# Shared-expert blocks ahead of the routing counts in a two-best expert stage

## Chip, cores and metric

One core of a Trainium2 chip runs the whole program. The metric is device time in microseconds of one execution. TensorE (PE), VectorE (DVE), ScalarE (ACT) and GpSimd (POOL) each run an instruction stream of their own and meet at semaphores; SyncE (SP) only issues transfers.

## What is computed

The program is an eight-block network on 2048 tokens of width 128. The change is inside its sixth block, a mixture of experts with the two best of eight experts for each token and one shared expert for all tokens. Cut to what matters:

```
logits = rms_normalised(x) @ router_w.T;  topk_p, topk_i = top_k(softmax(logits), 2)
rw     = topk_p / sum(topk_p)                         # the two weights of a token
sel    = tokens that chose an expert, in token order; capacity 320 a expert
eout   = (silu(xg @ rg) * (xg @ ru)) @ rd             # xg: the rows of an expert
routed = scatter-add of eout * weight back to the tokens
shared = (silu(x @ sg) * (x @ su)) @ sd               # sg, su: 128 x 1024, sd: 1024 x 128
out    = shared + routed                              # then x + out, layer norm
```

## The kernel before

`stage_top2_experts` (L2799) is one block of five hand-written streams, one to an engine, between two barriers. What order an engine works in is the order of its code; nothing is scheduled by a tool. `s.name` are semaphores that count up, and `at(i, c)` is the value after item c of turn i.

**Routing on DVE.** `choose` (lines L1943 to L1947) finds the best expert, then the second best, each as a chain of five small operations linked by a semaphore. `hot` (L3004) is the 0/1 table of choices, 128 partitions by 128 (expert, tile). PE multiplies it by two constant matrices (L2861, L2862, results in banks 2 and 1) and so gets each token's count within its expert. DVE turns the counts into slots (L1961, L1962, L3010 to L3014; the last one is `scatter`) and then into the weights (`gap`, `acc`, `share`, L3015 to L3026), for which POOL brings the reciprocal root `rms` and ACT one Exp (L2936).

**Rows by slot.** ACT copies the tokens into `x_with_id` (L2934, four copies of 128x1024). When `scatter` is there, POOL issues 32 indirect transfers (L3104), which send each token's row to its two slots in memory, and after every eighth it waits for those so far. SP then loads the rows back by expert (L3124, five transfers), POOL takes the row numbers out of them (`ids`, L3108) and PE transposes them (L2892, 20 products).

**The shared expert** works on pairs of 256-token batches, 512 tokens, pair i of four. A pair has eight blocks c. For a block, PE makes a gate product and an up product (L2881, 128x128 by 128x512) in banks 3 or 4 and 5 or 6, by c % 2. ACT applies Silu to the gate (`shared_gate`, L2948), DVE multiplies it by the up product (`shared_hid`, L3036). PE may start block c when DVE has done block c-2, since then the banks are free; block 0 of a pair waits for block 7 of the pair ahead. After blocks 0 and 1 of a pair, PE does `shared_down` of the pair ahead (L2872 and L2873, four groups) and ACT copies its results to `shared` (L2940). Three pairs (`FIRST = 3`) run before the row transposes and the routed experts (L2902, L2852), the fourth after them. Both wait forms are in two lines:

```
pe.wait_ge(s.s_hid.sem, s.s_hid.at(i, max(0, c - 1)))     # before the two products of block c
dve.wait_ge(s.s_silu.sem, s.s_silu.at(i, c + 1))          # before the multiplication of block c
```

PE begins with the count products, then the shared expert. ACT begins with the four copies, then the Exp, then Silu. DVE begins with all of the routing, weights included, and only then multiplies for the shared expert.

## Time and profile before

| | us |
|---|---|
| median of 3 runs (lowest, highest) | 1695.76 (1693.24, 1698.86) |
| the profiled execution, its own time | 1698.1 |
| its span, first to last instruction | 1696.3 |
| the changed block, in that span | 1316.2 to 1490.5 |
| PE busy in that block | 155.31 of 174.30 |

A row gives the time an instruction starts, how long it lasts, the engine and line, what it writes and reads, and in brackets how long its engine stood idle before it and who released it. PE rows of one product in 32-bit floats are two records (x2), and the next product may start before the last record's end, so the pace is read from start to start. The granted clock is a share of 2.4 GHz: 1.00 is 2.4 GHz, 0.50 is 1.2 GHz.

### The profile page before, as it was taken

What the parts mean: (1) busy time and instruction counts of PE and PEld (TensorE: products, weight loads), DVE (VectorE), ACT (ScalarE), POOL (GpSimd) and SP (SyncE); (2) the same over time, 40 slices, a digit from 0 to 9 for tenths busy, and PEclk for the clock granted to TensorE, in tenths of its full rate; (3) what the DMA queues carried; (4) which work ended last, traced back from release to release, by engine and by line L of the source; (5) the groups of instructions that cost most, each with busy time, mean ns of one, the idle gap of its engine ahead of it and who ended that gap; (6) DMA issues with size and microseconds to landing.
All of it is one profiled execution on the core that took longest, in us unless ns stands there. A gap on an engine that the chain in (4) does not pass through costs nothing. (4 is left out here: it accounts for less than half of the span.)

```text
span 1696.3 us, 30747 instructions
## 1 busy us (share of the span) xinstructions
PE 1483.6 (87%) x11059; PEld 1085.3 (64%) x11059; DVE 1009.1 (59%) x2372; ACT 854.9 (50%) x1876; POOL 672.6 (40%) x779
## 2 busy tenths in 40 slices
PE   4589999899887999996849999899998899879996
PEld 3256676566774677675737877877877467635554
DVE  6656647666476799994045554366645412546665
ACT  5455555655547877772524444544444323225552
POOL 3397715977133677872130000100003522123334
PEclk8789999999998899997959999999998899969998
DMA  7300000000204765616243000000000110200000
GB/s 217 98 14 14 13 14 1 14 13 19 89 1 62 87 73 81 80 41 139 74 126 93 1 1 1 1 2 1 1 1 1 35 48 20 62 4 2 2 2 26
DMA packets 80943, 66.58 MB, mean 39 GB/s; under 512 B 28283, under 2 KB 67242, under 8 KB 80814
## 3 DMA queue, kind: packets, MB, share of 16 engines
q1 hardware_dynamic: 71198, 57.24, 16.4%
q0 software_dynamic: 2688, 5.53, 1.1%
q10 hardware_dynamic: 6928, 2.12, 0.6%
q8 instruction: 78, 1.28, 0.3%
q14 instruction: 51, 0.42, 0.1%
HBM read 48.89 MB, written 11.71 MB: 36 GB/s over the span
## 5 line engine op out<-in xcount | busy, mean ns | idle before, releaser
L1557 POOL TENSOR_TENSOR inject<-delta_x,b_rows 128x512 f32<-128x512 f32 x128 | 160.2, 1277 | 65.1 <-DVE delta_x L1854 37.5
L1881 DVE TENSOR_TENSOR_SCAN state<-bank,inject 128x512 f32<-128x512 f32 x128 | 150.1, 1209 | 7.5 <-issue 5.2
L2314 POOL TENSOR_TENSOR ve<-mv,eps 128x1 f32<-128x1 f32 x32 | 6.1, 190 | 336.0 <-DVE mv L2462 336.0
L1786 ACT ACTIVATE bank<-delta,a_neg 128x255 f32<-128x255 f32 x256 | 108.9, 473 | 6.8 <-DVE state L1881 6.1
L2423 ACT ACTIVATE Z<-bank 128x512 f32<-128x512 f32 x64 | 34.7, 594 | 127.9 <-PE bank L2376 127.9
L2400 ACT ACTIVATE U<-bank 128x512 f32<-128x512 f32 x128 | 74.7, 593 | 41.1 <-PE bank L2337 40.1
L1661 PEld LDWEIGHTS bank<-tabs,by_token 128*128 128x128 f32 x512 | 68.7, 198 | 25.0 <-issue 15.1
L632 POOL TENSOR_TENSOR rotated<-rot_cos,rot_sin 128x512 f32<-128x512 f32 x52 | 65.8, 1269 | 46.0 <-DVE rot_sin L1001 46.0
L3613 DVE TENSOR_REDUCE top<-bank 128x2 f32<-128x512 f32 (+1 forms) x96 | 61.9, 686 | 35.6 <-PE bank L3317 17.8
L1797 ACT ACTIVATE by_token<-bank,c_cols 128x256 f32<-128x256 f32 x128 | 53.7, 470 | 50.5 <-PE bank L1635 50.2
L638 POOL TENSOR_TENSOR inv_norm<-sum_sq,neghalf 128x16 f32<-128x16 f32 x26 | 76.1, 2925 | 3.9 <-POOL sum_sq L636 0.8
L3214 POOL TENSOR_SCALAR_AFFINE_SELECT prob<-prob 128x512 f32<-128x512 f32 x64 | 39.1, 634 | 92.5 <-ACT prob L3519 92.5
L1665 PE MATMUL bank<-x_work,tabs 128*128 128x512 f32 x128 | 74.2, 663 | 0.0
L1661 PE MATMUL bank<-tabs,by_token 128*128 128x128 f32 x512 | 70.3, 282 | 0.0
L998 DVE TENSOR_TENSOR rot_cos<-bank,rope 128x512 f32<-128x512 f32 x64 | 43.9, 686 | 36.9 <-ACT squares L876 27.9
L3519 ACT ACTIVATE prob<-bank 128x384 f32<-128x384 f32 x128 | 53.2, 500 | 24.4 <-PE bank L3340 24.4
L681 PE MATMUL bank<-wqkv,hT 128*128 128x512 f32 x112 | 57.8, 641 | 8.4 <-ACT hT L871 6.2
L876 ACT ACTIVATE squares<-bank 128x512 f32<-128x512 f32 x64 | 38.1, 598 | 46.6 <-PE bank L681 20.7
L3036 DVE TENSOR_TENSOR shared_hid<-shared_gate,bank 128x512 f32<-128x512 f32 x32 | 21.9, 688 | 56.7 <-PE bank L2881 55.9
L906 ACT ACTIVATE prob<-bank 128x512 f32<-128x512 f32 x64 | 34.7, 595 | 40.9 <-PE bank L728 40.7
L643 POOL TENSOR_TENSOR rotated<-rotated,inv_norm 128x512 f32<-128x512 f32 x52 | 53.2, 1044 | 2.0
L1635 PE MATMUL bank<-tabs,state 128*128 128x128 f32 x256 | 40.4, 282 | 11.7 <-DVE state L1881 8.8
(575 smaller groups left out, 4126.7 us busy)
## 6 DMA issues: line engine op xcount, KB each, us to landing
b_rows<-rows_dram SPq DMA_DIRECT2D x32, 512.0 KB, 9.0
v<-v SPq DMA_DIRECT2D x32, 130.0 KB, 2.3
by_token<-zero SPq DMA_DIRECT2D x8, 256.0 KB, 3.3
moe_w<-in_L_ffn_rg_dram SPq DMA_DIRECT2D x1, 2048.0 KB, 8.4
moe_w<-in_L_ffn_ru_dram SPq DMA_DIRECT2D x1, 2048.0 KB, 13.7
x_with_id<-by_token SPq DMA_DIRECT2D x16, 128.0 KB, 2.4
wqkv<-in_L_ffn_wqkv_dram SPq DMA_DIRECT2D x2, 768.0 KB
rows<-padded SPq DMA_DIRECT2D x5, 258.0 KB, 4.6
```

The source lines that it names most:

```text
L632: pool.tensor_tensor(rot[:, p, m, :], rc[:, m % 2, :], rs[:, m % 2, :], ALU.add).then_inc(s.added.sem, 1)
L638: pool.tensor_tensor(flat(rn), flat(ss), net.neghalf[:, 0:2 * LH], ALU.pow).then_inc(s.inv_norm.sem, 2)
L643: pool.tensor_tensor(of, of, rn[:, m, :].unsqueeze(2).to_broadcast([P, LH, LDH]), ALU.mult).then_inc(s.roped.sem, 1)
L681: pe.matmul(to, hT[:, p, tok(t)], w[:, j * INNER:(j + 1) * INNER], start=True, stop=True).then_inc(s.qk_ps.sem, 1)
L1557: pool.tensor_tensor(dB[:, n % R, :, :], dx[:, :, seq(n)], both(b_all[:, q % 4, n % CH, :]), ALU.mult).then_inc(s.inject.sem, 1)
L1661: last = pe.matmul(sum_bank(i)[:, c * L + t * P:c * L + (t + 1) * P], hcT[:, j % RT, t, c * P:(c + 1) * P], ident, start=(k == 0 and t == ...
L1665: last = pe.matmul(sum_bank(i)[:, :], ident, flat(hc[:, j % R, :, :]), start=False, stop=(k == NS - 1))
L1786: last = act.activation(dA[n % RD][:, c, 1:L], delta[:, c, i * L + 1:(i + 1) * L], ACT.Exp, scale=a_neg[:, c, k:k + 1])
L1797: last = act.activation(hcT[:, j % RT, t, :], turn_bank[:, t * 2 * P:(t + 1) * 2 * P], ACT.Copy, scale=c_cols[:, TPB * i + t, k:k + 1])
L1881: dve.tensor_tensor_scan(flat(h[:, n % R, :, :]), flat(dA[n % RD]), flat(dB[:, n % R, :, :]), 0.0, ALU.mult, ALU.add).then_inc(s.state.sem, 1)
L2400: act.activation(U[:, m % 2, 4 * (g - 1):4 * g, :], bank[n % 2][:, :].rearrange("p (h t) -> p h t", h=4), ACT.Copy)\
L3613: dve.tensor_reduce(to, M[u % 2].rearrange("p (c k) -> p c k", c=count), AX.X, ALU.max).then_inc(s.maxed.sem, 1)
```

## The change

On PE the two count products move from the front of the stream to between block 1 and block 2 of pair 0. On ACT the four row copies move behind the Silu of block 1 of pair 0, and the Exp behind the Silu of block 0 of pair 1. On DVE the multiplications of pair 0 are put into the routing: blocks 0 and 1 behind `hot`, blocks 2 and 3 behind the counts, blocks 4 to 7 behind `scatter`, and the weights come after all of pair 0. No computation is added or removed.

```diff
@@ -2855,11 +2855,13 @@
             @block.tensor
             def _(pe):
                 pe.wait_ge(net.ld_w3, net.w3_ready)
-                pe.wait_ge(s.tables.sem, s.tables.at(0, 1))
-                pe.wait_ge(s.hot.sem, s.hot.at(0, 1))
-                flat = hot[:, :, :].rearrange("p e t -> p (e t)")
-                pe.matmul(bank[2][:, 0:NT * E2], ones[:, :], flat, start=True, stop=True)
-                pe.matmul(bank[1][:, 0:NT * E2], before[:, :], flat, start=True, stop=True).then_inc(s.counts.sem, 1)
+
+                def count():
+                    pe.wait_ge(s.tables.sem, s.tables.at(0, 1))
+                    pe.wait_ge(s.hot.sem, s.hot.at(0, 1))
+                    flat = hot[:, :, :].rearrange("p e t -> p (e t)")
+                    pe.matmul(bank[2][:, 0:NT * E2], ones[:, :], flat, start=True, stop=True)
+                    pe.matmul(bank[1][:, 0:NT * E2], before[:, :], flat, start=True, stop=True).then_inc(s.counts.sem, 1)
 
                 def shared_down(p):
                     pe.wait_ge(s.s_hid.sem, s.s_hid.at(p, SC))
@@ -2876,6 +2878,8 @@
                 def shared_expert(first, end):
                     for i in range(first, end):
                         for c in range(SC):
+                            if i == 0 and c == 2:
+                                count()
                             pe.wait_ge(s.s_hid.sem, s.s_hid.at(i, max(0, c - 1)))
                             for w, to, done in ((net.sg, gate_bank(c), s.sg_ps), (net.su, up_bank(c), s.su_ps)):
                                 pe.matmul(to[:, :], w[:, c * P:(c + 1) * P], net.xT[:, 2 * i * L:2 * (i + 1) * L], start=True, stop=True).then_inc(done.sem, 1)
@@ -2928,12 +2932,11 @@
 
             @block.scalar
             def _(act):
-                for half in range(2):
-                    for c in range(2):
-                        of = net.x_tok[:, half * T // 2:(half + 1) * T // 2].rearrange("p (t d) -> p t d", d=D)
-                        act.activation(with_id[:, c, half * NT // 2:(half + 1) * NT // 2, 0:D], of, ACT.Copy).then_inc(s.with_id.sem, 1)
-                act.wait_ge(s.shifted.sem, s.shifted.at(0, 1))
-                act.activation(gap[:, :], gap[:, :], ACT.Exp).then_inc(s.exp.sem, 1)
+                def number_rows():
+                    for half in range(2):
+                        for c in range(2):
+                            of = net.x_tok[:, half * T // 2:(half + 1) * T // 2].rearrange("p (t d) -> p t d", d=D)
+                            act.activation(with_id[:, c, half * NT // 2:(half + 1) * NT // 2, 0:D], of, ACT.Copy).then_inc(s.with_id.sem, 1)
 
                 def keep_shared(i):
                     act.wait_ge(s.shared_ps.sem, s.shared_ps.at(i, 1))
@@ -2946,6 +2949,11 @@
                             act.wait_ge(s.sg_ps.sem, s.sg_ps.at(i, c + 1))
                             act.wait_ge(s.s_hid.sem, s.s_hid.at(i, max(0, c - 1)))
                             act.activation(sgate[:, c % 2, :], gate_bank(c)[:, :], ACT.Silu).then_inc(s.s_silu.sem, 1)
+                            if i == 0 and c == 1:
+                                number_rows()
+                            if i == 1 and c == 0:
+                                act.wait_ge(s.shifted.sem, s.shifted.at(0, 1))
+                                act.activation(gap[:, :], gap[:, :], ACT.Exp).then_inc(s.exp.sem, 1)
                             if c == 1 and i > first:
                                 keep_shared(2 * i - 2)
                                 keep_shared(2 * i - 1)
@@ -2993,6 +3001,14 @@
                     ins.then_inc(s.v.sem, 1)
                     dve.wait_ge(s.v.sem, s.v.at(0, count[0]))
 
+                def shared_pair(i, first=0, end=SC):
+                    for c in range(first, end):
+                        dve.wait_ge(s.s_silu.sem, s.s_silu.at(i, c + 1))
+                        dve.wait_ge(s.su_ps.sem, s.su_ps.at(i, c + 1))
+                        if i >= 2:
+                            dve.wait_ge(s.shared_ps.sem, s.shared_ps.at(2 * (i - 1), 0))
+                        dve.tensor_tensor(shid[:, i % 2, c, :], sgate[:, c % 2, :], up_bank(c)[:, :], ALU.mult).then_inc(s.s_hid.sem, 1)
+
                 count_tables(dve, link, net, before[:, :], ones[:, :], keep[:, :, :], E2)
                 dve.nop().then_inc(s.tables.sem, 1)
                 by_tile = lambda ap: ap.rearrange("p e t -> p t e")
@@ -3002,16 +3018,19 @@
                 link(dve.scalar_tensor_tensor(rest[:, :, :], hot1, NEG, logits, ALU.mult, ALU.add))
                 choose(dve, link, rest[:, :, :], iota, tops[:, 1, :], eq[:, :, :], index[:, 1, :], hot2, E2)
                 dve.tensor_tensor(hot[:, :, :], hots[:, 0, :, :], hots[:, 1, :, :], ALU.add).then_inc(s.hot.sem, 1)
+                shared_pair(0, 0, 2)
                 trash = net.tab("trash").rearrange("p (k t) -> p k t", k=2)
                 link(dve.tensor_scalar(offset[:, :, :], index[:, :, :], float(C2), float(64 * C2 - 1), ALU.mult, ALU.add))
                 link(dve.tensor_tensor(offset[:, :, :], offset[:, :, :], trash, ALU.subtract))
                 dve.wait_ge(s.counts.sem, s.counts.at(0, 1))
                 counts_before(dve, link, pre[:, :, :], keep[:, :, :], bank[1][:, 0:NT * E2], bank[2][:, 0:NT * E2])
+                shared_pair(0, 2, 4)
                 link(dve.tensor_tensor(at_hot[:, :, :, :], hots[:, :, :, :], pre[:, :, :].unsqueeze(1).to_broadcast([P, 2, E2, NT]), ALU.mult))
                 link(dve.tensor_reduce(pos[:, :, :], at_hot[:, :, :, :].rearrange("p k e t -> p k t e"), AX.X, ALU.add))
                 link(dve.tensor_tensor(slot[:, :, :], pos[:, :, :], offset[:, :, :], ALU.add))
                 link(dve.scalar_tensor_tensor(offset[:, :, :], pos[:, :, :], float(C2), slot[:, :, :], ALU.is_le, ALU.mult))
                 dve.tensor_tensor(scatter[:, :, :], offset[:, :, :], trash, ALU.add).then_inc(s.slots.sem, 1)
+                shared_pair(0, 4, SC)
                 link(dve.tensor_tensor(gap[:, :], tops[:, 1, :], tops[:, 0, :], ALU.subtract))
                 link(dve.tensor_scalar(acc[:, :, :], pos[:, :, :], float(C2), None, ALU.is_le))
 
@@ -3026,16 +3045,7 @@
                     link(dve.tensor_tensor(p2, inv[:, :], acc[:, 1, :], ALU.mult))
 
                 weights()
-
-                def shared_pair(i, first=0, end=SC):
-                    for c in range(first, end):
-                        dve.wait_ge(s.s_silu.sem, s.s_silu.at(i, c + 1))
-                        dve.wait_ge(s.su_ps.sem, s.su_ps.at(i, c + 1))
-                        if i >= 2:
-                            dve.wait_ge(s.shared_ps.sem, s.shared_ps.at(2 * (i - 1), 0))
-                        dve.tensor_tensor(shid[:, i % 2, c, :], sgate[:, c % 2, :], up_bank(c)[:, :], ALU.mult).then_inc(s.s_hid.sem, 1)
-
-                for i in range(FIRST):
+                for i in range(1, FIRST):
                     shared_pair(i)
                 for e in range(E2):
                     for c in range(FC):
```

ScalarE holds one table of functions at a time; where the order of functions changes, the compiler places the loads (ACT_TABLE_LOAD) anew. Below, the start of the block on ACT before, in program order. `x_with_id` are the row copies, `gap` the Exp.

```order
L2934 ACTIVATE x_with_id<-x_tok 128x8x128 x4
L2936 ACTIVATE gap<-gap 128x16
L2948 ACT_TABLE_LOAD
L2948 ACTIVATE shared_gate<-bank 128x512 x10
L2940 ACTIVATE shared<-bank 128x256 x2
```

And the same place of the changed kernel:

```order
L2951 ACT_TABLE_LOAD
L2951 ACTIVATE shared_gate<-bank 128x512 x2
L2939 ACTIVATE x_with_id<-x_tok 128x8x128 x4
L2951 ACTIVATE shared_gate<-bank 128x512 x7
L2956 ACT_TABLE_LOAD
L2956 ACTIVATE gap<-gap 128x16
L2951 ACT_TABLE_LOAD
L2951 ACTIVATE shared_gate<-bank 128x512
L2943 ACTIVATE shared<-bank 128x256 x2
```

One table load has become three: the first stands at the very start of the block, the other two enclose the Exp, between blocks 0 and 1 of pair 1.

On PE, the start of the block in the changed kernel (before, L2861 and L2862 stood ahead of the first product of L2881):

```order
L2885 MATMUL bank<-xT,sg 128x512
L2885 MATMUL bank<-xT,su 128x512
L2885 MATMUL bank<-xT,sg 128x512
L2885 MATMUL bank<-xT,su 128x512
L2863 MATMUL bank<-hot,ones_158 128x128
L2864 MATMUL bank<-hot,before 128x128
L2885 MATMUL bank<-xT,sg 128x512
L2885 MATMUL bank<-xT,su 128x512
```

Four products of pair 0 now stand ahead of the counts, which still wait for `hot`.

On DVE, from `hot` on in the changed kernel (before, L3036, the multiplication, came only behind the last `share`, 24 times in a row):

```order
L3020 TENSOR_TENSOR hot<-hots 128x128
L3010 TENSOR_TENSOR shared_hid<-shared_gate,bank 128x512 x2
L3023 TENSOR_SCALAR offset<-index 128x32
L3024 TENSOR_TENSOR offset<-offset,tabs 128x32
L1961 SCALAR_TENSOR_TENSOR pre<-keep,bank 128x128
L1962 TENSOR_TENSOR pre<-pre,bank 128x128
L3010 TENSOR_TENSOR shared_hid<-shared_gate,bank 128x512 x2
L3028 TENSOR_TENSOR at_hot<-hots,pre 128x256
...
L3032 TENSOR_TENSOR scatter<-offset,tabs 128x32
L3010 TENSOR_TENSOR shared_hid<-shared_gate,bank 128x512 x4
L3034 TENSOR_TENSOR gap<-tops 128x16
```

Four multiplications now stand ahead of `scatter`, and all eight of pair 0 ahead of the weights.

## Rows read from the trace of the kernel before

**Rows 1.** The page: span, and busy time of each engine.

```profile
span 1696.3 us, 30747 instructions
PE 1483.6 (87%) x11059; PEld 1085.3 (64%) x11059; DVE 1009.1 (59%) x2372; ACT 854.9 (50%) x1876; POOL 672.6 (40%) x779
```

**Rows 2.** Busy time of the engines and granted clock (PEclk), by stretches.

```profile
core 0: us, PE busy (x) PEld busy (x) DVE busy (x) ACT busy (x) POOL busy (x), PEclk, DMA share, GB/s
1316.20:1321.70 5.50, 0.00 (x0) 0.02 (x1) 4.66 (x19) 3.90 (x4) 3.25 (x2) 0.50 0.00 0
1321.70:1324.50 2.80, 2.79 (x5) 1.30 (x6) 2.28 (x7) 0.00 (x0) 0.00 (x0) 0.50 0.00 0
1324.50:1326.70 2.20, 2.20 (x6) 0.77 (x4) 1.59 (x9) 1.45 (x2) 1.14 (x1) 0.99 0.00 0
```

**Rows 3.** Timeline of PE: the block's start, pair 0, start of pair 1.

```profile
1321.71 0.27 PE L2861 MATMUL bank<-hot,ones 128*128 128x128 bf16 x1 [5.73 <-DVE hot L3004]
1321.87 2.02 PE L2881 MATMUL bank<-xT,sg 128*128 128x512 f32 x2
1323.69 1.46 PE L2881 MATMUL bank<-xT,su 128*128 128x512 f32 x2
1324.98 1.02 PE L2881 MATMUL bank<-xT,sg 128*128 128x512 f32 x2
1325.84 1.02 PE L2881 MATMUL bank<-xT,su 128*128 128x512 f32 x2
1328.19 1.13 PE L2881 MATMUL bank<-xT,sg 128*128 128x512 f32 x2 [1.33 <-DVE shared_hid L3036]
...
1339.61 1.12 PE L2881 MATMUL bank<-xT,sg 128*128 128x512 f32 x2 [0.85 <-DVE shared_hid L3036]
```

**Rows 4.** Timeline of ACT: the block's start.

```profile
1316.26 3.90 ACT L2934 ACTIVATE x_with_id<-x_tok 128x1024 f32<-128x1024 f32 x4 [0.77 <-PEq L2727]
1325.24 0.22 ACT L2936 ACTIVATE gap<-gap 128x16 f32<-128x16 f32 x1 [5.08 <-DVE gap L3020]
1325.47 1.28 ACT L2948 ACT_TABLE_LOAD   x1
1326.76 1.08 ACT L2948 ACTIVATE shared_gate<-bank 128x512 f32<-128x512 f32 x2
```

**Rows 5.** Timeline of DVE: from hot to the first multiplications.

```profile
1321.27 0.29 DVE L3004 TENSOR_TENSOR hot<-hots 128x128 bf16<-128x128 f32 x1
1322.19 0.42 DVE L1961 TENSOR_TENSOR_SCAN pre<-keep,bank 128x128 f32<-128x128 f32 x1 [0.31 <-PE bank L2862]
1322.97 0.42 DVE L3010 TENSOR_TENSOR at_hot<-hots,pre 128x256 f32<-128x256 f32 x1
1324.50 0.19 DVE L3014 TENSOR_TENSOR scatter<-offset,tabs 128x32 int32<-128x32 f32 x1
1327.45 1.28 DVE L3036 TENSOR_TENSOR shared_hid<-shared_gate,bank 128x512 f32<-128x512 f32 x2 [0.88 <-ACT shared_gate L2948]
```

**Rows 6.** Timeline of the next block's start, ACT and weight loads of PE.

```profile
1490.50 1.28 ACT L3493 ACT_TABLE_LOAD   x1 [0.27 <-PEq L2842]
1490.51 0.50 PEld L3280 LDWEIGHTS bank<-w_qkv,xT 128*128 128x128 f32 x2 [1.10 <-issue]
```

**Rows 7.** Timeline of PE: down products of pair 0, end of the third pair.

```profile
1343.15 1.95 PE L2872 MATMUL bank<-sd,shared_hid 128*128 128x128 f32 x16
...
1351.19 1.02 PE L2881 MATMUL bank<-xT,sg 128*128 128x512 f32 x2
...
1393.52 2.35 PE L2892 MATMUL bank<-tabs,rows 128*128 128x128 f32 x20
```

**Rows 8.** Timeline of POOL: first of 32 scatters, last, last row numbers.

```profile
1325.55 1.14 POOL L3104 DMA_INDIRECT padded<-x_with_id,scatter  x1 [4.58 <-DVE scatter L3014]
...
1368.77 0.96 POOL L3104 DMA_INDIRECT padded<-x_with_id,scatter  x1 [0.30 <-issue]
...
1379.67 0.19 POOL L3108 CAST ids<-rows 128x4 int32<-128x4 f32 x1 [0.65 <-DMA rows<-padded]
```

## The prediction, made before the change was run

> **What bounds the kernel now.** I read the page first: PE is busy for 1483.6 of 1696.3 us and is the busiest engine [rows 1], so a change pays if it closes a gap on PE and leaves PE's work as it is. Then the busy time by stretches at the start of the changed block. From 1316.2 to 1321.7 PE does nothing, while DVE is busy for 4.66 us with the choice of experts and ACT for 3.90 us with its copies; the granted clock is 0.50, the 1.2 GHz level [rows 2]. PE's timeline says what ends this: `hot`, after 5.73 us of idle [rows 3]. The next gap follows soon. The four products of blocks 0 and 1 begin at 1321.87, the last at 1325.84 and, at the pace of 0.86 us, it is done at 1326.70; then PE stands until 1328.19, waiting for `shared_hid` [rows 3]. ACT's timeline has the cause: Exp must wait for the routing until 1325.24, the Silu table comes behind it, and the first Silu starts at 1326.76 [rows 4]. From 1328.19 on PE works evenly: pair 1 starts at 1339.61 [rows 3], which is 11.42 us for the six blocks 2 to 7 and the hand-over to the next pair. A block is a gate and an up product of 0.86 us each; two blocks are 3.43 us of it, so four blocks with the hand-over are 7.99 us.
>
> Behind that the cover of the routed rows counts: PE wants them only at 1393.52 [rows 7], while the last row numbers are there at 1379.67 [rows 8]. There are 13.8 us of room.
>
> The number to follow through the change is therefore the start of pair 1. What it moves forward, the rest of the block should pass on: from there to the row transposes PE is the engine waited for.
>
> **PE, the first four products.** They no longer wait for `hot`. In the next block PE loads its first weights at 1490.51, with ACT's first instruction at 1490.50 [rows 6]; so I let PE start here with ACT, at about 1316.3 [rows 4]. Their length hangs on the clock. In the kernel before, PE starts at the low level; over its first 2.80 us the granted clock is 0.50, and in the next 2.20 us it is 0.99 [rows 2], which makes the four products last 4.83 us (1321.87 to 1326.70). When the rise comes if PE starts 5.5 us sooner, the trace doesn't show. The bounds: again 2.8 us after the start, so that they end at 1321.1; or not at all within them, so that all four run at twice 0.86 us, with the 0.1 us more that the first row shows, and end at 1323.2.
>
> **The counts.** `hot` ends at 1321.56 (1321.27 and 0.29), as before, since nothing ahead of it on DVE is touched. At the first bound PE waits for it for some 0.5 us, and the counts come at the same time as now. At the second bound they come 1.5 us later than now.
>
> **ACT.** The Silu table is loaded at once, 1316.3 to 1317.5 (1.28 us [rows 4]), and the first gate product ends at 1318.1 at the earliest, so this load is hidden. The Silu of block 1 needs the third product: it is done at 1321.1, at the second bound at 1322.3. Then come the four copies, 3.90 us [rows 4]: ACT is free for block 2 at 1325.0 or 1326.2. This is the new wait. Behind the copies on ACT stands the Silu of block 2, behind that its multiplication on DVE, behind that block 4 on PE, and the at_hot to `scatter` chain.
>
> **DVE.** Two multiplications of 1.28 us together [rows 5] end at 1322.9, two offset operations take 0.4, the count operations 0.78 (1322.19 to 1322.97 [rows 5]): 1324.1. Then DVE waits for ACT. Silu of block 2 takes 0.6 (1.08 for two, 0.48 apart), the multiplication 0.7 with its 0.1 us of hand-over: `shared_hid` of block 2 is there at 1326.4, at the second bound at 1327.6.
>
> **Sum for pair 0.** PE starts block 2 at 1322.3 when block 0 has been multiplied, blocks 2 and 3 take 3.4 us to 1325.8, then it stands 0.6 us and starts block 4 at 1326.4. Four blocks and the hand-over are 7.99 us, so pair 1 starts at 1334.4 in place of 1339.61: 5.2 us gained. At the second bound it is 1327.6 + 8.0 = 1335.6 and 4.0 us. Put as gaps: 5.7 us at `hot` and 1.5 us at the table go, 1.0 to 1.1 us come back at the copies and before the counts, and what the slow clock takes longer is the difference between the bounds.
>
> If the clock rises sooner than 2.8 us, the Silu of block 1 comes before 1321.1 and everything behind it too; the copies then end at 1324.2 or so, and the gain goes to about 5.9 us. I take 4.7 us, a little above the middle of 4.0 and 5.2, for that side.
>
> **Scatter.** The two further multiplications, blocks 2 and 3, now stand ahead of it. Block 3's ends at 1327.0; the chain from at_hot to `scatter` takes 1.72 us (1322.97 to 1324.69 [rows 5]), so `scatter` is ready at 1328.8 or, at the second bound, 1329.9, which is 4.1 to 5.2 us late. All 32 scatters of POOL move with it, and the five loads on SP's queue and the row numbers behind them: the last are there at 1384 to 1385. PE wants them at 1393.52 less the gain, 1388.8. Four to five of the 13.8 us of room are left; without them each us of lateness would cost one.
>
> **Exp and weights.** After pair 0 on DVE, at about 1334.4, `gap` needs some 0.6 us; ACT does the Silu of block 0 of pair 1 until about 1336.1, then a load, Exp at 0.22 and a load: 1338.9, and the Silu of block 1 ends at 1339.5. DVE's five weight operations, queued ahead of the multiplications of pair 1, end at about 1339.0, so block 1 is multiplied by 1340.3. PE has blocks 0 and 1 and then 8.04 us of down products (1343.15 to 1351.19 [rows 7]), now until 1346.0. The 2.8 us that ACT adds are hidden with 5.7 us to spare; without this cover they would cost 2.8 us.
>
> This is where a rule speaks against the change. The Trainium skill, page "ScalarE: Activation LUTs", section "What ACT_TABLE_LOAD costs", puts a switch at 2.66 us, with 1.38 us of draining on top of the load, and its rules for kernel authors ask for grouping by table. Here Exp ends at 1325.46, the load runs from 1325.47 to 1326.75 and Silu starts at 1326.76 [rows 4]: no draining shows. By the page the two loads around Exp would take 5.3 us in place of 2.6, the cover would shrink from 5.7 to 3.0 us, and the sum would be the same.
>
> **The sum.** The profiled execution took 1698.1 us, its span 1696.3 and 1.8 around it; less 4.7 that is 1693.4. It lies 2.3 us above the median of the runs, so against the median I forecast 1695.76 - 4.7 = 1691.1 us. The three runs lie 5.6 us apart, as much as the whole gain.
>
> **Rivals.** (a) As summed, gain 4.0 to 5.9 us, 1689.9 to 1691.8 us: 75%.
> (b) The change does less than it says, since the gain is swallowed behind pair 1 or PE does not really start with ACT: gain 0 to 3.5 us, time about 1694. For it: the room for the rows shrinks from 13.8 to about 4 us, and what else might hold PE at the block's start is hidden now by the wait for `hot`. Against it: the start of the next block, and the even pace of the scatters: 13%.
> (c) The gaps cost less than the rows of before suggest (copies overlap with Silu, clock up at once, later steps also gain): 6 to 7.5 us, about 1689: 7%.
> (d) Slower. The clock stays at the low level through all of pair 0, because PE now starts in the cold and then pauses at `hot`, at block 4 and at the hand-over. Twelve products after block 1, each 0.86 us longer, are 10.3 us; less the gain at the second bound of 4.0 that is 6.3 us lost, 1702. It turns the sign once the low level lasts over five of these products. Against it: the clock of before holds through the pause of 1.49 us at 1326.70, which the pace of 0.86 us afterwards shows: 5%.
>
> **Range and chances.** A change of 0.3%, 5.1 us, is about what a measurement tells from none; the border lies at 1690.7 and my forecast is just on the near side. Case (a) is split by it and by the spread of the runs, about 38 of its 75 points beyond the border and 37 within; (c) is faster; (b) is within; of (d) 4 points are slower. So 0.46 faster, 0.50 the same, 0.04 slower. For the range I take (a) and add the spread of a median of few runs, some 2 us each way, and the near part of (b) and (c): 1687.3 to 1694.8.
>
> **What the changed profile would show.** PE idle at the start under 0.5 us; the table load first on ACT; count products at 1321.7 to 1323.3 in place of 1321.71; PE waiting for `shared_hid` about 0.6 us before block 4; first scatter 4 to 5 us later; two table loads around Exp with no wait of PE behind; PE without a wait at the row transposes; pair 1 started at 1334.4 to 1335.6 and the block shorter by as much. The prediction is wrong if pair 1 starts sooner but the row transposes do not, if PE's first product starts well after ACT's first instruction, or if the granted clock is 0.50 beyond block 1.

## The result: 3.6 us less, and what the profile after shows

The changed kernel takes 1693.18 us, the median of 17 runs (1689.24 to 1695.32); the kernel before takes 1695.87 us in 17 runs (1693.09 to 1700.24). The ratio is 0.9979, with a 95% interval of 0.9971 to 0.9987: 3.6 us less, between 2.2 and 4.9. The two medians lie only 2.7 us apart, the two means 3.5; the gains given here by the ratio are not differences of medians. The forecast was 4.7 us less. Measured again (`e6_after_again` below) the ratio was 0.9971, 0.9957 to 0.9984, or 4.9 us less.

The profiled execution of after took 1689.24 us. The page's lines, beside [rows 1]:

```profile
span 1687.5 us, 30750 instructions
PE 1484.6 (88%) x11059; PEld 1085.6 (64%) x11059; DVE 1008.8 (60%) x2372; ACT 857.0 (51%) x1878; POOL 672.6 (40%) x779
```

PE has the same 11059 matmul records and is busy 1 us longer; ACT has the two table loads more and is busy 2.1 us longer. The span is 8.8 us shorter, and this must not be put down to the change: ACT's first instruction of the changed block stands at 1311.18, against 1316.26 before [rows 4], so 5.1 us of it were won ahead of any line that the change touches. In the profiles of this study the block begins anywhere from 1310.89 to 1318.72, with the same code ahead of it. So from here on each time in the block is read as a **distance from ACT's first instruction of the block**. The timeline of ACT, to be laid beside [rows 4] and, with its last line, [rows 6]:

```profile
1311.18 1.28 ACT L2951 ACT_TABLE_LOAD   x1 [0.81 <-PEq L2727]
1313.47 0.60 ACT L2951 ACTIVATE shared_gate<-bank 128x512 f32<-128x512 f32 x1 [1.01 <-PE bank L2885]
1316.59 0.60 ACT L2951 ACTIVATE shared_gate<-bank 128x512 f32<-128x512 f32 x1 [2.52 <-PE bank L2885]
1317.08 3.88 ACT L2939 ACTIVATE x_with_id<-x_tok 128x1024 f32<-128x1024 f32 x4
1320.87 1.07 ACT L2951 ACTIVATE shared_gate<-bank 128x512 f32<-128x512 f32 x2
...
1332.04 1.28 ACT L2956 ACT_TABLE_LOAD   x1
1333.34 0.21 ACT L2956 ACTIVATE gap<-gap 128x16 f32<-128x16 f32 x1
1333.57 1.28 ACT L2951 ACT_TABLE_LOAD   x1
1334.87 0.60 ACT L2951 ACTIVATE shared_gate<-bank 128x512 f32<-128x512 f32 x1
...
1481.15 1.28 ACT L3503 ACT_TABLE_LOAD   x1 [0.27 <-PEq L2842]
```

The load is the first thing on ACT now, and is over before the first gate product is. Between Silu of blocks 1 and 2 stand the four copies; until 1320.87 ACT can't take up block 2. The last line is the next block's first instruction: the block lasts 169.97 us in place of 174.24 [rows 4, 6], 4.27 less. PE's timeline, beside [rows 3, 7]:

```profile
1311.39 2.04 PE L2885 MATMUL bank<-xT,sg 128*128 128x512 f32 x2 [0.53 <-PEq L2727]
1313.23 1.91 PE L2885 MATMUL bank<-xT,su 128*128 128x512 f32 x2
1314.94 1.61 PE L2885 MATMUL bank<-xT,sg 128*128 128x512 f32 x2
1316.39 1.02 PE L2885 MATMUL bank<-xT,su 128*128 128x512 f32 x2
1317.24 0.22 PE L2863 MATMUL bank<-hot,ones 128*128 128x128 bf16 x1
...
1322.28 1.12 PE L2885 MATMUL bank<-xT,sg 128*128 128x512 f32 x2 [1.27 <-DVE shared_hid L3010]
...
1330.27 1.12 PE L2885 MATMUL bank<-xT,sg 128*128 128x512 f32 x2 [0.85 <-DVE shared_hid L3010]
...
1333.80 1.95 PE L2874 MATMUL bank<-sd,shared_hid 128*128 128x128 f32 x16
...
1341.84 1.02 PE L2885 MATMUL bank<-xT,sg 128*128 128x512 f32 x2
...
1384.17 2.35 PE L2896 MATMUL bank<-tabs,rows 128*128 128x128 f32 x20
```

The idle time in brackets on the first line is 0.53 us in place of 5.73. Read the starts of the next four lines against each other: 1.84, 1.71, 1.45 and 0.85 us apart, so PE goes from the slow pace to the fast one within the third product. After blocks 2 and 3 it waits 1.27 us for `shared_hid`: that is the wait put there by the copies. Pair 1 starts at 1330.27. The busy time by stretches (columns as in [rows 2]) has the clock to it:

```profile
1311.20:1315.70 4.50, 4.31 (x5) 1.83 (x6) 3.84 (x15) 1.86 (x2) 3.10 (x2) 0.50 0.00 0
1315.70:1317.30 1.60, 1.60 (x5) 0.67 (x4) 1.27 (x4) 0.71 (x2) 0.15 (x1) 0.87 0.00 0
1317.30:1322.20 4.90, 3.71 (x11) 1.45 (x9) 2.34 (x7) 4.64 (x6) 0.00 (x0) 1.00 0.00 0
```

The low level (0.50, 1.2 GHz) holds for all of the first row and, at a mean of 0.87, for 0.42 us of the second, so until 1316.12. That is 4.7 us after PE's start, where it was 2.8 us before [rows 2]; then comes 2.4 GHz, which stays through the wait at block 4. DVE and POOL, beside [rows 5, 8]:

```profile
1316.15 0.29 DVE L3020 TENSOR_TENSOR hot<-hots 128x128 bf16<-128x128 f32 x1
...
1317.52 0.69 DVE L3010 TENSOR_TENSOR shared_hid<-shared_gate,bank 128x512 f32<-128x512 f32 x1 [0.49 <-PE bank L2885]
...
1321.54 1.28 DVE L3010 TENSOR_TENSOR shared_hid<-shared_gate,bank 128x512 f32<-128x512 f32 x2 [2.24 <-ACT shared_gate L2951]
...
1324.27 0.19 DVE L3032 TENSOR_TENSOR scatter<-offset,tabs 128x32 int32<-128x32 f32 x1
```

```profile
1325.32 1.14 POOL L3114 DMA_INDIRECT padded<-x_with_id,scatter  x1 [9.46 <-DVE scatter L3032]
...
1378.01 0.19 POOL L3118 CAST ids<-rows 128x4 int32<-128x4 f32 x1 [0.64 <-DMA rows<-padded]
```

As distances, with the same rows of before:

| distance from ACT's first instruction, us | before | after | earlier by |
|---|---|---|---|
| PE's first product of block 0 | 5.61 | 0.21 | 5.40 |
| block 2 starts | 11.93 | 6.18 | 5.75 |
| block 4 starts | 15.47 | 11.10 | 4.37 |
| pair 1 starts | 23.35 | 19.09 | 4.26 |
| row transposes start | 77.26 | 72.99 | 4.27 |
| next block starts | 174.24 | 169.97 | 4.27 |
| first scatter | 9.29 | 14.14 | -4.85 |
| last row numbers | 63.41 | 66.83 | -3.42 |

The gain is 5.4 to 5.8 us while PE fills its idle time, loses 1.4 us in front of block 4, and from pair 1 on is carried without loss to the end of the block. Behind the block part of it is given back. From the next block's first instruction to the end of the span the kernel before has 205.80, 205.80 and 205.84 us in three profiles (with `e5` and `e9` below), the changed one 206.35 and 206.31 (with `e6`): 0.5 us more, with the same code. The granted clock over the first 50 us of this stretch is 0.75 in all three profiles of before and 0.70 in both of after. So 3.7 to 3.8 us of the 4.3 reach the end of the kernel, which fits the 3.6 of the ratio. That the clock costs these 0.5 us is not shown: `e7` has 0.80 there and yet 206.08 us.

### The profile page after: what moved, and what is told of

Its sections match the earlier page's. It is cut to its first block and busy times, and to the rows that moved or that the text cites. A ratio compares the mean times of both kernels' runs of the same rounds, so it can differ in the third digit from the quotient of the medians.

```text
span 1687.5 us, 30750 instructions
## 1 busy us (share of the span) xinstructions
PE 1484.6 (88%) x11059; PEld 1085.6 (64%) x11059; DVE 1008.8 (60%) x2372; ACT 857.0 (51%) x1878; POOL 672.6 (40%) x779
## 3 DMA queue, kind: packets, MB, share of 16 engines
q8 instruction: 78, 1.28, 0.3%
```

## The experiments

Theory A is the forecast's: the gain is PE's idle time at the block's start, less the wait at the copies, less what the low clock costs, with enough cover for the rows and for Exp. The rivals are that the gain is given back behind pair 1, by rows that come too late or by what ACT has to do there, or that one part of the change makes all of it. In the expectations of `e5` to `e9`, theories A and B are something else: whether a stop of ACT that the first four profiles show comes with the chip (A) or with the new orders (B). The kernels ran in three groups, each on one chip: the first four, then `e5` to `e8`, then `e9` to `e12`. Diffs are against the changed kernel.

**The first four** try each order by itself. `e1_counts_only` has PE's order of the changed kernel and leaves ACT's and DVE's as they were before:

```diff
             def _(act):
-                def number_rows():
+                for half in range(2):
...
+                act.wait_ge(s.shifted.sem, s.shifted.at(0, 1))
+                act.activation(gap[:, :], gap[:, :], ACT.Exp).then_inc(s.exp.sem, 1)
...
                 dve.tensor_tensor(hot[:, :, :], hots[:, 0, :, :], hots[:, 1, :, :], ALU.add).then_inc(s.hot.sem, 1)
-                shared_pair(0, 0, 2)
...
-                shared_pair(0, 2, 4)
...
-                shared_pair(0, 4, SC)
...
                 weights()
-                for i in range(1, FIRST):
+                for i in range(FIRST):
                     shared_pair(i)
```

> Only PE's stream is changed (four products of pair 0 ahead of the counts); ACT and DVE work in the order of before. Measure: the distance from ACT's first instruction of the block to the first product of pair 1, 23.35 us before and 19.09 us in the changed kernel. Theory (the idle time of PE at the start is worth nothing by itself, since block 2 waits for the first multiplication, which needs Silu, its table, Exp and the routing): distance 23.4 to 24.0, time as before or up to 0.7 us more, since the counts now wait for four products at the low clock. Rival (what counts is that PE's 5.7 us of idle time are filled): distance about 18, time 5 us less than before.

`e2_copies_two_and_two` makes two of the copies behind Silu of block 0 and two behind block 1:

```diff
-                def number_rows():
-                    for half in range(2):
+                def number_rows(halves):
+                    for half in halves:
...
-                            if i == 0 and c == 1:
-                                number_rows()
+                            if i == 0 and c < 2:
+                                number_rows((c,))
```

> The changed kernel, but ACT makes two of its four row copies behind the Silu of block 0, where it stood idle for 2.5 us, and two behind the Silu of block 1. Theory (the four copies in a row make PE wait 1.4 us at block 4): no wait of PE at block 4, distance 17.7 us (19.09 less 1.4), 1.4 us less than the changed kernel and 5.7 us less than before, ratio to before 0.9967. Rival (PE waits there for the multiplication behind the routing on DVE, or the slow clock is the bound): distance 19.1, the time of the changed kernel.

`e3_copies_first` has all four ahead of the first Silu, as before:

```diff
-                            if i == 0 and c == 1:
-                                number_rows()
...
+                number_rows()
                 shared_expert(0, FIRST)
```

> The changed kernel, but all four row copies ahead of the first Silu, and so ahead of its table load too. Theory (position of the copies): Silu of block 0 comes only 5.2 us after the block's start, block 2 begins 0.5 us later than in the changed kernel, but block 4 does not wait: distance 18.1 us, 1.0 us less than the changed kernel. Rival (copies don't matter): 19.1.

`e4_exp_in_pair_0` has Exp and the weights where half of pair 0 still has to be done, so that no down products cover the two table loads:

```diff
-                            if i == 1 and c == 0:
+                            if i == 0 and c == 3:
                                 act.wait_ge(s.shifted.sem, s.shifted.at(0, 1))
...
-                shared_pair(0, 4, SC)
                 link(dve.tensor_tensor(gap[:, :], tops[:, 1, :], tops[:, 0, :], ALU.subtract))
...
                 weights()
+                shared_pair(0, 4, SC)
```

> The changed kernel, but the weights on DVE come straight behind scatter, ahead of the multiplications of blocks 4 to 7, and Exp on ACT behind the Silu of block 3: the two table loads lose their cover of down products. Theory (loads of 1.28 us each, hidden only by that cover): Exp at 14.0 us from the start, Silu of block 4 at 15.5, block 6 on PE at 16.9 in place of 14.6: distance 21.4 us, 2.3 us more than the changed kernel. Rival 1 (a switch costs 2.66 us): 22.8 us. Rival 2 (the place of Exp does not matter): 19.1 us.

Measured, with the start of pair 1 as a distance:

| kernel | pair 1 | transposes | block | median, us | ratio to before |
|---|---|---|---|---|---|
| e1_counts_only | 25.84 | 81.34 | 178.31 | 1699.81 | 0.9964 (0.9950 to 0.9979) |
| e2_copies_two_and_two | 17.49 | 82.42 | 179.4 | 1699.83 | 0.9962 (0.9947 to 0.9978) |
| e3_copies_first | 18.0 | 81.32 | 178.29 | 1702.58 | 0.9980 (0.9963 to 0.9998) |
| e4_exp_in_pair_0 | 21.43 | 83.09 | 180.06 | 1699.90 | 0.9959 (0.9944 to 0.9974) |

The starts of pair 1 can be read; the rest can't. Those of `e2`, `e3` and `e4` are within some 0.2 us of what was expected; that of `e1`, 25.84, lies outside both its theory and its rival, and is taken up again with `e10`. Here the kernel before took 1705.96 us, 10 more than elsewhere, and in all four profiles the stretch from pair 1 to the transposes is 55.5 to 64.9 us long, where it is 53.9 in the profiles of before and after. ACT's and then PE's timeline of `e2_copies_two_and_two` show where:

```profile
1340.40 0.38 ACT L2943 ACTIVATE shared<-bank 128x256 f32<-128x256 f32 x1 [2.67 <-PE bank L2875]
1349.14 0.38 ACT L2943 ACTIVATE shared<-bank 128x256 f32<-128x256 f32 x1 [8.36 <-remote]
1350.58 0.60 ACT L2951 ACTIVATE shared_gate<-bank 128x512 f32<-128x512 f32 x1 [1.05 <-remote]
```

```profile
1344.10 1.02 PE L2885 MATMUL bank<-xT,sg 128*128 128x512 f32 x2
...
1352.10 2.08 PE L2885 MATMUL bank<-xT,sg 128*128 128x512 f32 x2 [4.40 <-DVE shared_hid L3010]
```

PE is done with all down products at 1344.10, and yet ACT takes up the last of their results only at 1349.14; `remote` is the trace's word for a releaser that it doesn't see. PE then waits 4.40 us and works on at the slow pace. Two explanations were open: a new order on ACT brings this about (theory B), or it belongs to the chip. So the kernels were run again elsewhere, beside unchanged ones.

**The changed kernel and the one before, again.** `e5_before_again` is the kernel before, `e6_after_again` the changed one, without an edit.

> The kernel before, unchanged, profiled again beside the others of this call. In the profiles of the first four experiments ACT stood still for 5 us or more around the copies of the shared results of pair 0, with PE's products long done, and the kernel before took 1706 us there against 1696 in its first runs. Theory A (this comes with the chip or the moment, not with the order of the work): the kernel before shows the same stop on such a chip, in the stretch from pair 1 to the row transposes, 53.9 us in its first profile and then about 60. Theory B (the changed orders bring it about): 53.9 us here, whatever the chip.

> The changed kernel, unchanged, again. Distance from ACT's first instruction of the block to the first product of pair 1: 19.1 us where the clock rises about 4.3 us after PE's start, 18.2 us if it rises after 2.8 us or less, 19.3 us if later. Time against before: by the distances 4.3 us less, ratio 0.9975. Theory A of the stop in ACT: from pair 1 to the transposes the same length as the kernel before has in this call. Theory B: longer than there.

Before: pair 1 at 23.35, transposes at 77.26, block 174.24 us, in one run of 1694.70 us. After: pair 1 at 19.00, transposes at 72.91, block 169.89, median 1692.90 against 1696.44, ratio 0.9971 (0.9957 to 0.9984). Between these profiles and the first ones PE's distances repeat to 0.1 us, while the whole kernel's time wanders by 5. So the gain in the block, 4.27 to 4.35 us, is known better from two pairs of profiles than from the timed runs. The clock rises 4.7 us after PE's start here too, and not after the expectation's 4.3, where the first row of the stretches above ends. The kernel before shows no stop of ACT on this chip, so theory A of the stop is left untried.

**Copies two and two, again.** `e7_copies_two_and_two_again` is the code of `e2`.

> Copies two and two, again. Distance 17.5 us as in the first look. By the distances 5.9 us less than before, ratio 0.9966, and 1.6 us less than the changed kernel of the same call. Theory B of the stop (an order that keeps ACT's copies away from block 4 brings it about): from pair 1 to the transposes 60 us or more where the changed kernel has 54.

Pair 1 starts at 17.34, the transposes at 71.26, the block lasts 168.24 us; median 1691.09, ratio 0.9960 (0.9947 to 0.9973). The stretch behind pair 1 is 53.92 us long again: ACT's long stop is gone with the same code, so the order alone does not cause it. ACT's timeline, then PE's:

```profile
1321.09 2.00 ACT L2939 ACTIVATE x_with_id<-x_tok 128x1024 f32<-128x1024 f32 x2
1323.47 0.60 ACT L2951 ACTIVATE shared_gate<-bank 128x512 f32<-128x512 f32 x1 [0.39 <-PE bank L2885]
1323.97 1.99 ACT L2939 ACTIVATE x_with_id<-x_tok 128x1024 f32<-128x1024 f32 x2
1325.86 0.59 ACT L2951 ACTIVATE shared_gate<-bank 128x512 f32<-128x512 f32 x1
```

```profile
1324.31 1.13 PE L2885 MATMUL bank<-xT,sg 128*128 128x512 f32 x2
...
1327.84 1.02 PE L2885 MATMUL bank<-xT,sg 128*128 128x512 f32 x2
```

The first two copies lie where ACT waits for the third product, 2.52 us in the changed kernel. Block 4 starts at 1327.84 with no wait in brackets. This version beats both kernels: 6.8 us below before by the ratio, 6.0 by the length of the block, 1.65 of it over the change. Of the 1.65, 0.16 are there at block 2 already, where the clock had risen 4.3 us after PE's start and not 4.7; some 1.5 us are the place of the copies.

**The rows made late.** `e8_late_scatter` does six more multiplications on DVE ahead of the chain from `at_hot` to `scatter`, and Exp one block later:

```diff
                 shared_pair(0, 2, 4)
+                shared_pair(0, 4, SC)
+                shared_pair(1, 0, 2)
                 link(dve.tensor_tensor(at_hot[:, :, :, :], ...
...
-                shared_pair(0, 4, SC)
...
                 weights()
+                shared_pair(1, 2, SC)
-                for i in range(1, FIRST):
+                for i in range(2, FIRST):
```

> The changed kernel, but the chain from at_hot to scatter and the weights on DVE come behind the multiplications of pair 0 and of blocks 0 and 1 of pair 1, and Exp on ACT behind the Silu of block 1 of pair 1: the first scatter is issued about 12 us later than in the changed kernel. Theory (room for the rows in the changed kernel: the last row numbers are there 6.2 us ahead of the first transpose and some 8 ahead of the last four): pair 1 starts as in the changed kernel, the transposes wait, and the experts begin 4 us later than in the changed kernel, so that the gain over before is gone. Rival (the room is larger, the rows are wanted later): no difference.

The first scatter stands at 25.90 in place of 14.05, the last row numbers at 78.34 in place of 67.05. Pair 1 starts at 18.9 as in `e6`, but the first transposes come at 74.34 (72.91) and the routed experts at 80.17 (76.15), 4.0 us later, as expected. PE's timeline there:

```profile
1389.41 0.64 PE L2896 MATMUL bank<-tabs,rows 128*128 128x128 f32 x4 [1.36 <-DMA rows<-padded]
1390.38 0.66 PE L2896 MATMUL bank<-tabs,rows 128*128 128x128 f32 x4 [0.33 <-DMA rows<-padded]
1391.56 3.00 PE L2896 MATMUL bank<-tabs,rows 128*128 128x128 f32 x12 [0.52 <-DMA rows<-padded]
```

Before, 20 transposes stood in one line without a wait [rows 7]; now they come in pieces and wait for the loaded rows. The block lasts 173.91 us (174.24 before) and the ratio is 0.9998 (0.9987 to 1.0008): of the 4.35 us 0.33 are left. So without room for the rows the change would not pay. The changed kernel leaves 72.99 - 66.83 = 6.2 us of it, of 13.9 before.

**The kernel before, a third time,** as a measure for the last group:

> The kernel before, profiled beside the others of this call: distance 23.35 us, pair 1 to row transposes 53.9 us as in its first two profiles; if ACT stops on this chip as it did in the first four experiments, about 60 us here too (theory A) or 53.9 still (theory B, the changed orders bring it about).

Pair 1 at 23.34, block 174.23 us, 1696.74 us. Nothing has moved.

**PE's order alone, again.** `e10_counts_only_again` is the code of `e1`.

> Only PE's order changed, again, since its first look (distance 25.8 us, longer than before) and its first time (6 us less than before) contradict each other. Theory: PE works for some 5.5 us, then stands for 6 us, in which the clock falls back to the low level, and blocks 2 and 3 run at it: distance 25.8 us, 2.5 us slower than before, ratio 1.0015. If the clock holds, 23.9 us and 0.5 us slower. Rival (the filled idle time counts): faster than before by 3 us or more.

Median 1699.02, ratio 1.0022 (1.0010 to 1.0034): some 3.7 us slower, though PE's idle time at the start is filled just as in the changed kernel. PE's timeline:

```profile
1312.20 2.05 PE L2885 MATMUL bank<-xT,sg 128*128 128x512 f32 x2 [0.45 <-PEq L2727]
...
1318.01 0.22 PE L2863 MATMUL bank<-hot,ones 128*128 128x128 bf16 x1
...
1324.39 2.08 PE L2885 MATMUL bank<-xT,sg 128*128 128x512 f32 x2 [6.11 <-DVE shared_hid L3040]
1326.26 1.92 PE L2885 MATMUL bank<-xT,su 128*128 128x512 f32 x2
1327.97 1.91 PE L2885 MATMUL bank<-xT,sg 128*128 128x512 f32 x2
1329.68 1.43 PE L2885 MATMUL bank<-xT,su 128*128 128x512 f32 x2
```

The 5.73 us of idle are not removed; they have become 6.11 us two blocks later, because the first multiplication still stands behind the whole routing. And three more products and part of a fourth run at the slow pace, 1.87, 1.71, 1.71 and 1.27 us from start to start, for the granted clock has fallen back to 0.50 in the wait. Pair 1 starts at 26.8, 3.5 us later than before and 1.0 later than expected. `e1`, the same code, gave 25.84 with the same picture: its clock rose 3.2 us after PE's start where this one took 4.6, which is 0.54 us by block 2, and the second slow stretch is 0.4 us shorter. Yet the timed ratio of `e1`, 0.9964, is on the other side of 1 with an interval that doesn't touch this one: the reason why nothing here is built on the times of the first group.

**Exp in pair 0, again.** `e11_exp_in_pair_0_again` is the code of `e4`.

> Weights and Exp inside pair 0, again. Distance 21.4 us as in the first look, 2.4 us slower than the changed kernel and 1.9 us faster than before, ratio to before 0.9989. Rival (the place of Exp doesn't matter for the time): ratio 0.9974.

Pair 1 starts at 21.31 (21.43 in `e4`), the block lasts 172.21 us, median 1695.16, ratio 0.9985 (0.9971 to 0.9999). This interval holds the rival's 0.9974 too; it is the distance that speaks against the rival. ACT's timeline, then PE's:

```profile
1325.61 1.28 ACT L2956 ACT_TABLE_LOAD   x1
1328.66 0.22 ACT L2956 ACTIVATE gap<-gap 128x16 f32<-128x16 f32 x1 [1.76 <-DVE gap L3038]
1328.89 1.28 ACT L2951 ACT_TABLE_LOAD   x1
1330.18 1.08 ACT L2951 ACTIVATE shared_gate<-bank 128x512 f32<-128x512 f32 x2
```

```profile
1331.61 1.12 PE L2885 MATMUL bank<-xT,sg 128*128 128x512 f32 x2 [1.98 <-DVE shared_hid L3010]
```

Without the down products as cover, this place of Exp costs 2.3 us: 21.31 less 19.00 in `e6`. The first load doesn't wait for `gap`, only the Exp does, 1.76 us longer than the load lasts. So the first load costs nothing here, and the 2.3 us are that wait, the Exp and the second load, less what PE had in hand. The second load takes 1.28 us, and from its start to the Silu behind it are 1.29. The Trainium skill, page "ScalarE: Activation LUTs", section "What ACT_TABLE_LOAD costs", puts a switch at 2.66 us; an estimate from this figure, with 1.4 us more at the second load, would have set pair 1 at about 22.8. `e4` (21.43) and `e11` (21.31) disagree with it, and the measurement decides.

**One block ahead in place of two.** `e12_one_block_ahead` is `e7` with the counts between blocks 0 and 1:

```diff
-                            if i == 0 and c == 2:
+                            if i == 0 and c == 1:
                                 count()
```

> Copies two and two, but the counts come after block 0 already, so that only two products stand ahead of them. Theory (both blocks ahead of the counts are worth their time): PE stands from 3.7 to 5.5 us, makes block 1 only then, at 0.86 or 1.7 us a product, and starts block 2 at 7.3 to 9.0 us in place of 5.9: distance 18.7 to 20.4 us, 1.4 to 3.1 us more than copies two and two. Rival (the wait for hot hides it, one block is enough): 17.4 us.

Pair 1 starts at 18.61, 1.3 us later than in `e7` and just under the expected range, the block lasts 169.50 us, ratio 0.9984 (0.9972 to 0.9997). PE's timeline:

```profile
1320.78 1.92 PE L2885 MATMUL bank<-xT,su 128*128 128x512 f32 x2
1324.13 0.22 PE L2863 MATMUL bank<-hot,ones 128*128 128x128 bf16 x1 [1.44 <-DVE hot L3020]
1324.24 1.07 PE L2885 MATMUL bank<-xT,sg 128*128 128x512 f32 x2
```

PE waits 1.44 us for `hot`. The two products ahead of this wait ran at the slow pace; the granted clock rises within the wait, 4.3 us after PE's start, and PE goes on at the fast pace. With one block ahead of the counts the new orders together bring 4.7 us (23.34 less 18.61), and the second block adds 1.3.

## Why the prediction was right, and where its sizes were off

**Reading distances to the start of pair 1** was the right number to follow: 4.26 us earlier there, 4.27 at the transposes and at the next block. The forecast took 4.7 between the bounds 4.0 and 5.2. The intervals of the timed gains, 3.6 (2.2 to 4.9) and 4.9 (2.7 to 7.3, by the ratio's interval), both hold the 4.3 of the block. The result lies within the range, and within 0.3% of before, the side to which the forecast gave the larger chance by little. The time alone would not have decided for the forecast's mechanism: 1693.18 us is outside the 1689.9 to 1691.8 of case (a) and nearer to the 1694 of rival (b). It is the distances inside the block that decide.

**Behind the block** the forecast put nothing. The runs show 0.5 us given back there, so at the kernel's end the gain is 3.7 to 3.8 us, below the 4.0 of its second bound.

**The list of gaps** in the prediction doesn't add up: 5.7 and 1.5 less 1.1 is 6.1, not the 5.2 of its first bound. Its chain of times, on which the forecast rests, has 5.4 and 1.5 gained, and 1.0 lost ahead of block 2 and 0.6 at block 4. The slip changed nothing in the forecast.

**PE, the first four products.** It starts 0.21 us behind ACT, as taken. Of the clock, the first bound (a rise 2.8 us after the start) didn't come: there were 4.7 us of low level, and the products ended 6.06 us after ACT's first instruction, where the bounds gave 4.8 and 6.9. This is the mis-sized term, and the others hang on it.

**The counts** were thought to wait 0.5 us for `hot`, or to come 1.5 us late. `hot` was there at 1316.44, the counts ran at 1317.24: no wait of PE, and as a distance 0.6 us later than before.

**ACT.** The load is hidden and the copies take 3.88 us. As the third product was slow for most of its time, Silu of block 1 ran from 1316.59 to 1317.19 and was done 6.0 us into the block; the bounds gave 4.8 and 6.0. ACT was free for block 2 at 9.7, against 8.7 and 9.9.

**The new wait** was where it was said to be, at block 4 behind the copies, but 1.27 us long in the trace and 1.4 as the prediction counts it, by the pace, and not 0.6. The sum has 0.6 at the first bound and 0.8 at the second, and the measured wait is longer than both, because the clock rose within the third product: that made ACT late, as at the second bound, while the fourth product was fast and PE was through with blocks 2 and 3 early, nearly as at the first. With block 4 at 11.10, against 10.1 and 11.3 by the bounds, plus the 7.99 us, one has the 19.09 measured. Taking the value on the side of the earlier rise was the choice that went wrong; the two bounds for the gain held, and `e7` shows that the place of the copies cost some 1.5 us.

**Scatter** came 4.85 us later (4.1 to 5.2 forecast); the room left for the rows is 6.2 us, not 4 to 5, because the last row numbers moved by 3.4 us only. They repeat less well than PE's starts: 62.60 to 63.41 in three profiles of before, 66.83 and 67.05 after, so that by other pairs they moved by up to 4.5, and the room before was 13.9 to 14.7 us. That the room was worth watching, `e8` shows: 11.3 us later row numbers cost 4.0 us, nearly the whole gain.

**Exp and weights** are hidden: the loads at 1332.04 and 1333.57 leave no wait of PE behind them, the down products run from 1333.80 to 1341.84. The price without cover was put at 2.8 us, as two loads and the Exp. The two uncovered cases have 2.3, but of other parts: one load lies in the wait for `gap`, and this wait is in the price. So they don't measure the 2.8.

**Rival (b),** gain swallowed behind pair 1, falls: every us that pair 1 had gained was there at the next block, in the change, in `e6`, `e7`, `e11` and `e12`. **Rival (c),** a gain of 6 us or more, falls by the same distances. **Rival (d),** a clock that stays low, falls for the changed kernel, where the clock holds in a wait of 1.27 us. Its mechanism is real, as `e10` shows after a wait of 6.11 us, and there it makes the kernel slower. It was sound to keep it as a rival, and its price was set too high, at twelve slow products; in `e10` there are three and part of a fourth.

**Which part brings what.** PE's order alone costs 3.5 us at pair 1 in `e10`, 2.5 in `e1`. With the new orders of ACT and DVE as well it brings 4.3. Those two belong together: a multiplication ahead of the weights needs a Silu ahead of the Exp, since the Exp waits for `gap` behind it. What they bring while PE keeps its old order was not run, so that PE's order is needed for the gain is argued and not shown; an estimate from the rows of before is that they could close at most the 1.5 us in front of block 2. The copies' place takes some 1.5 us off again, and could be had better by `e7` or, at 18.0 against 19.09 at pair 1, even by leaving them first (`e3`, whose later part can't be read).

**Left open:** what makes the rest of the kernel 0.5 us longer behind the changed block, and what held ACT up to 8 us in the first group. The kernel before has no profile from that chip, so whether it had the same stop isn't shown, only that it took 10 us more there.

## What to carry to other kernels

Idle time that is filled ahead of a wait is worth only what the consumers of the filling can drain: follow the buffers to the engine that frees them, and move its work too. When a transfer moves later to make place, measure its room first (here 13.9 us, 6.2 left), since past it the gain goes: row numbers 11.3 us later cost 4.0. For a gain of 0.3% or less, compare distances from the block's own first instruction: here most repeat to 0.1 or 0.2 us, where whole runs spread over 5. They do so only where the clock rises at the same place (`e1` and `e10`, one code, are 1.0 us apart), and the stretch behind the block has to be compared too.

## What was not expected of the hardware

The low clock level lasted 2.8 us from PE's start in three profiles of the kernel before [rows 2], 4.7 in both of the changed one, and 3.2 and 4.6 in `e1` and `e10`, one code; what sets it wasn't found. Waits of PE of 1.27 us (after) and 1.98 us (`e11`) left the fast pace, waits of 4.40 us (`e2`) and 6.11 us (`e10`) brought back the slow one. With the same code behind the block, the granted clock over the next 50 us was 0.75 before and 0.70 after, each time again. The time of the part ahead of the block differs by up to 8 us between executions of the same code. And one chip ran the kernel before at 1706 us, where two others had 1696.4 and 1696.6, with stops of ACT of up to 8.36 us whose releaser the trace doesn't name.
